# The attention layer's VectorE order: the weighted values of tile t ahead of the low part of tile t-1

## The reference

```python
q = (rowEmb @ qTrans).reshape(-1, HEADS, head_dim)
k = (colEmb @ kTrans).reshape(-1, HEADS, head_dim)
v = (colEmb @ vTrans).reshape(-1, HEADS, head_dim)
att = jnp.clip(jnp.einsum('ehd,ehd->eh', q, k), -10.0, 10.0)
expAtt = jnp.exp(att)
attNorm = segment_sum(expAtt, rows)[rows]
att = expAtt / (attNorm + 1e-08)
out = segment_sum((att[:, :, None] * v).reshape(-1, EMB), rows)
```

## Time and profile before

| | |
|---|---|
| median of 3 runs | 1238.45 us (1238.22 to 1241.88) |
| the profiled execution | 1255.07 us |
| its span, first to last instruction | 1253.3 us |
| attention tiles, first VectorE one-hot to the joining of the sums | 703.5 to 958.4 us |
| TensorE busy | 967.4 us, 77% |
| VectorE busy | 961.5 us, 77% |
| ScalarE busy | 600.1 us, 48% |
| GpSimd busy | 662.5 us, 53% |

### The profile page before, as it was taken

The page is one execution under the profiler, slowest core; times in us unless marked ns, Lnnn a source line. Parts: engine busy times, 40 slices in busy tenths (PEclk is TensorE's granted clock), DMA queues, the critical chain, the costliest instruction groups (busy, mean ns, idle before and its releaser), DMA issues.

```text
span 1253.3 us, 32626 instructions
## 1 busy us (share of the span) xinstructions
PE 967.4 (77%) x12003; PEld 732.8 (58%) x12003; DVE 961.5 (77%) x1247; ACT 600.1 (48%) x1503; POOL 662.5 (53%) x446
## 2 busy tenths in 40 slices
PE   4967577887999999999994767877772777727773
PEld 3645456776444544545543667877772777727763
DVE  8887878888565555565446499999998689978996
ACT  5531027777111111111101477878784389838984
POOL 1008888888788888888788889988100000000000
PEclk9977786555999999999995688888896589978998
DMA  8643214555222222222303388777834877728774
GB/s 167 130 104 74 53 28 165 191 191 153 57 71 69 83 70 69 83 70 83 67 2 111 117 275 276 265 270 267 301 137 172 341 289 282 279 83 291 282 299 137
DMA packets 73565, 202.18 MB, mean 161 GB/s; under 512 B 36667, under 2 KB 37467, under 8 KB 73509
## 3 DMA queue, kind: packets, MB, share of 16 engines
q1 hardware_dynamic: 57300, 186.25, 41.3%
q10 hardware_dynamic: 2465, 13.60, 4.8%
q0 software_dynamic: 13744, 1.59, 4.1%
HBM read 155.30 MB, written 45.63 MB: 160 GB/s over the span
## 4 chain that ended last, share of the span: by engine, by line
PE 42%; DVE 34%; issue 15%; DMA 4%; ACT 3%; DVEq 2%; SPq 0%; ACTq 0%
PE ps L1640 24%; DVE arena L982 4%; PE ps L1592 4%; DVE arena L948 4%; DVE arena L936 4%; DVE arena L957 3%; PE ps L1495 2%; DVE arena L1032 2%; PE ps L1452 2%; DVE arena L962 2%; PE ps L1437 2%; DMA base_room<-ohd_table 2%; DVE h_room L962 2%; PE ps L1482 2%; DMA hl_room<-in_edge_attr_dram 2%
## 5 line engine op out<-in xcount | busy, mean ns | idle before, releaser
L561 POOL DMA_INDIRECT w_table<-wpa,slot_i x425 | 657.1, 1546 | 218.3 <-issue 218.3
L1640 PE MATMUL ps<-arena,hl_room 125*128 125x500 f16 (+1 forms) x1750 | 342.7, 352 | 2.6 <-DVE hl_room L1218 2.0
L1437 PE MATMUL ps<-arena 125*128 125x64 f16 (+1 forms) x3900 | 232.0, 211 | 87.4 <-ACT arena L606 52.5
L1640 PEld LDWEIGHTS ps<-arena,hl_room 125*128 125x128 f16 x1750 | 155.7, 97 | 162.6 <-issue 4.6
L1437 PEld LDWEIGHTS ps<-arena 125*128 125x128 bf16 x3900 | 178.8, 103 | 93.4 <-ACT arena L606 50.5
L701 ACT ACTIVATE part_room<-ps 128x500 f16<-128x500 f32 (+1 forms) x70 | 38.0, 543 | 306.6 <-PE ps L1640 247.4
L1227 DVE SCALAR_TENSOR_TENSOR part_room<-ps,part_room 128x500 f16<-128x500 f32 (+1 forms) x70 | 43.6, 622 | 149.2 <-ACT part_room L701 143.6
L1442 PE MATMUL ps<-arena 125*128 (+1 forms) x1300 | 136.1, 205 | 0.0
L606 ACT ACTIVATE arena<-ps 128x384 f32<-128x384 f32 x325 | 130.9, 504 | 7.9 <-PE ps L1442 6.2
L632 ACT ACTIVATE arena<-ps,part_room 128x64 f32<-128x64 f32 x500 | 107.9, 339 | 18.6 <-PE ps L1437 10.9
L1442 PEld LDWEIGHTS ps<-arena 125*128 125x128 bf16 x1300 | 114.7, 108 | 0.5
(11 more groups left out here) (266 smaller groups left out, 1468.6 us busy)
## 6 DMA issues: line engine op xcount, KB each, us to landing
hl_room<-slot_rows SPq DMA_DIRECT2D x49, 832.0 KB, 4.3
arena<-slot_rows SPq DMA_DIRECT2D x38, 832.0 KB, 15.8
arena<-ohd_table SPq DMA_DIRECT2D x26, 832.0 KB, 5.0
arena<-ohs_table SPq DMA_DIRECT2D x25, 832.0 KB
base_room<-ohd_table SPq DMA_DIRECT2D x24, 832.0 KB, 5.9
hl_room<-in_edge_attr_dram ACTq DMA_DIRECT2D x17, 750.0 KB
ohs_table<-xs_room SPq DMA_DIRECT2D x25, 448.0 KB
ohs_table<-xs_room SPq DMA_DIRECT2D x25, 384.0 KB
```

Of the source, the lines that this page charges most:

```text
L561: pool.indirect_dma_start(w_table, bass.IndirectOffsetOnAxis(slot_i[:, u:u + 1], 0), wpa[:, u], None).then_inc(S[f"w_out{g % 2}"], 16)
L1437: last = pe.matmul(ps[:, m % RING, o:o + b - a], slots[:, k * L:(k + 1) * L], rhs, start=(i == 0), stop=(i == 1))
L1640: last = pe.matmul(ps[:, c, 0:w], hl[0:P, u, s, :], adj[:, s, c * CH * P:c * CH * P + w], start=(s == 0), stop=(s == T - 1))
```

## The change

In `layer1`, the four lines of the low part move from ahead of the weighted values to behind them. After the clamp of tile t, VectorE now comes first to the weighted values of tile t, with their waits for `l1_exp` and `l1_low`, and then to the low part of tile t-1, with its wait for `l1_high`. No instruction is added or removed, all waits keep their values, and no other engine's code changes.

```diff
                         vec.tensor_scalar(logit, logit, bound[:, 0:1], bound[:, 1:2], ALU.max, ALU.min).then_inc(S["l1_logit"], 1)
-                    if 3 in on:
-                        vec.wait_ge(S["l1_high"], s - 2)
-                        vec.scalar_tensor_tensor(msg1[:, 1 - par, :, M1:], msg1[:, 1 - par, :, 0:M1], HSCALE, G1m[1 - par],
-                                                 ALU.mult, ALU.subtract).then_inc(S["l1_low"], 1)
                     if 2 in on:
                         vec.wait_ge(S["l1_exp"], s - 1)
                         vec.wait_ge(S["l1_low"], s - 1)
                         vec.tensor_tensor(G1m[par][:, :, 0:D].rearrange("p c (a d) -> p c a d", a=HEADS),
                                           G1[:, par, :, D:2 * D].rearrange("p c (a d) -> p c a d", a=HEADS),
                                           exps.unsqueeze(3).to_broadcast([L, C, HEADS, HD]), ALU.mult
                                           ).then_inc(S["l1_val"], 1)
+                    if 3 in on:
+                        vec.wait_ge(S["l1_high"], s - 2)
+                        vec.scalar_tensor_tensor(msg1[:, 1 - par, :, M1:], msg1[:, 1 - par, :, 0:M1], HSCALE, G1m[1 - par],
+                                                 ALU.mult, ALU.subtract).then_inc(S["l1_low"], 1)
```

## The result

The changed kernel is slower. Its median over five runs is 1252.91 us (1249.60 to 1256.35), that of the kernel before, over five runs with the first three among them, 1241.88 us (1238.22 to 1244.62). The ratio is 1.0087, with a 95% interval of 1.0052 to 1.0121, about 11 us. The forecast was 12.0 us more, 1.0%, at 1250.4 us in a range of 1246.5 to 1254.

What follows compares the result with a forecast made beforehand. VectorE was taken to bound the kernel: 23 exposed waits of 0.53 us give 12.2 us, less 0.2 in the tail, so 12.0 on the median of 1238.45, 1250.4 us. The ends were 1247.5 to 1251.6, widened to 1246.5 to 1254.

Steps and rivals of the forecast that it cites:

- the tail: After step 26's clamp: the last low part comes 1.3 us earlier, but two back-to-back scatters on TensorE leave 0.2 us returned.
- the sum: 23 waits, 12.2 us, less 0.2 us returned at the end: 12.0 us, added to the median of 1238.45 us.
- The full engine: VectorE, busy 203.56 of 205 us at 9.55 us a step: a wait put into its sequence has nothing to hide in.
- The exposed wait: VectorE after each clamp: weighted values start after 0.78 us instead of 0.25, so 0.53 us a step, 12.2 us over 23.
- The covers: In the loop: the later low part keeps 3.2 us of slack before its scatter, and the product's row copies end in time.
- The bound of 1.3: Microseconds returned after the last clamp if TensorE were not in the way; used for the range's lower end, 1247.5 us.
- The profiled total: The whole profiled execution should go from 1255.07 to about 1267 us.
- rival 1: At the clamp on VectorE: the wait is covered after all, kernel not slower, 1237.2 to 1238.3 us; chance 0.03.
- mild form: At the clamp: some 0.2 of the 0.53 us come from profiling, leaving 7.4 us, so 1245.9 us; chance 0.06.
- rival 3: Low part late for its scatter, gathers and row copies set the step; several microseconds a step, above 1300 us; chance 0.02.
- rival 2: GpSimd comes first in the gap after the clamp: 0.66 us more in 16 steps, 10.6 at most, 1261.0 us; chance 0.05.

Runs made afterwards that it cites:

- e1: Kernel before, old order, with one added wait for the exponential ahead of the low part, nothing moved; ratio 1.0119 to the kernel before.
- e4: Changed kernel with the exponential computed twice by ScalarE, the first into an unused tile; ratio 1.0138 to the kernel before.
- e2: Changed kernel with the second one-hot moved from ahead of the clamp to between clamp and weighted values; ratio 1.0019 to the kernel before.
- e3: Kernel before, with the new order in step 26 alone, the last with weighted values; ratio 0.9998 to the kernel before.
- e6: e3 plus 140 unused matmuls on TensorE ahead of the last two scatters; 1237.92 us, ratio 0.9965 to the kernel before.
- e7: Changed kernel plus 100 unused matmuls on TensorE ahead of the last two scatters; ratio 1.0065 to the kernel before.
- e5: Kernel before, old order, with the exponential computed twice by ScalarE, the first into an unused tile; ratio 1.0020 to the kernel before.

## Why the prediction was right

The direction, the cause and the size of the wait held, and one term, the tail, did not. The kernel was 11.0 us slower where 12.0 were forecast, and the forecast ratio of 1.0097 lies in the measured interval. The time of 1252.91 us lies in the range only because this was widened for noise: it is above 1251.6, the upper end that the sum gave, since the three runs to which the sum was added had a median 3.43 us below that of all five. Point by point:

**The full engine.** Every step lost what was put into VectorE's sequence, and every run with another addition paid for it in the same way (0.53 in e1, 0.27 in e4, 0.12 in e2). Nothing absorbed it.

**The exposed wait.** 0.78 us from clamp to weighted values was read from step 2 and came out as 0.78 in all steps. From step 2's clamp to step 26's the time went from 947.00 - 721.50 = 225.50 us to 942.96 - 705.11 = 237.85, 12.35 more against 12.2.

**The covers.** ScalarE's idle before the high part vanished as said, and no wait of TensorE for the low part appeared in the loop. The low part ends at 817.94 + 2.00 = 819.94 and the scatter that needs it starts at 822.54:

```profile
822.54 1.70 PE L1452 MATMUL ps<-arena 128*128 128x136 f16 x26
```

That is 2.6 us of slack, where 3.2 were worked out from another step's scatter. One scatter was too few: in the loop's steps the slack runs from 1.41 us (low part done at 809.86, scatter at 811.27) to 3.11, and in the kernel before from 3.8 to 5.4, of which the prediction read one, 4.96. The cover held, with less than half of the margin that was claimed for it.

**The tail** is the term that was mis-sized: 0.2 us were to come back, and it was 11.35 - 10.18 = 1.17. The order of events was as described, down to the two scatters back to back. The step that failed put 3.11 us on each of them, from rows at the 1.2 GHz level; the second, which began near 950.6, was granted 0.97 of full speed from 951.6 to 952.8, and the pair took 5.15 us in place of 6.22. In e3, where both stayed near the lower level, the tail gave 0.30, and with both at the higher level 8.65 us remain. The bound of 1.3 that was kept for the range covered 1.17 by luck: it stood for a TensorE that is not in the way, and it is no bound either, as e6 and e7 give back 2.70, the 1.3 and the 1.41 by which a scatter is shorter at the higher level (3.11 - 1.70). By the prediction's own terms the 0.2 is 0.1 (951.67 + 6.22 = 957.89 against 958.00), which changes nothing.

**The profiled total** did not go to about 1267. Adding the sum to one profiled execution assumed that the next one would spend the same time in the earlier stages, and the next one reached L1640 12.9 us earlier and step 2's clamp 721.50 - 705.11 = 16.39 us earlier. What could be tested in the profile was the stage, and the sum there came out at 11.2 against 12.0.

**The rivals.** A covered wait (rival 1) is excluded by the step of 10.08 us. Its mild form, that profiling stretches the hand-over, would give 7.4 us, a ratio of 1.0060, which the interval of the changed kernel still holds. What speaks against it is e1, where 24 x 0.33 = 7.9 us would be 1.0064 and the interval begins at 1.0083. A late scatter (rival 3) did not occur. GpSimd (rival 2) did not hold up the weighted values: the steps are 10.08 us while its DMAs run and after their end at 825. It seems to hold up VectorE a little, though: in e2 the step is 9.71 us while its indirect DMAs run, 9.75 in the step of its last instruction at 823, and 9.67 behind it, and the one-hot behind the clamp takes 1.11 to 1.12 us, then 1.16, then 1.08:

```profile
881.26 0.33 DVE L952 TENSOR_SCALAR arena<-arena,bound 128x104 f32<-128x104 f32 x1
881.51 1.08 DVE L936 TENSOR_SCALAR arena<-arena,lane 125x3328 bf16<-125x3328 bf16 x1
882.51 1.88 DVE L958 TENSOR_TENSOR arena<-arena 128x1664 f32<-128x1664 f32 x1
```

If that is the mechanism of rival 2, it is worth 0.04 us a step and not the 0.66 that bounded it. The Trainium skill, "SBUF — State Buffer", section "Who interferes with whom", says of VectorE's two-port modes that whoever issues first gets the port pair shared with GpSimd for the whole instruction. No run here shows VectorE waiting for the 1.19 us that a GpSimd instruction takes when undisturbed.

## What to carry to other kernels

On an engine that is full, an instruction between a producer's hand-over and the use of what comes back is a cover, and its price is known before it is moved: the round trip from the start of the handed-over instruction to the start of the user, less the step to the next instruction. A step of the same loop that lacks the cover, here step 2, often shows that round trip already. Where TensorE idles ahead of the last matmuls of a stage, price them at both clock levels, as bounds, and compare profiles by the stage, not by their totals.

## What the runs showed of the hardware beyond this

In the changed kernel GpSimd also got through its work sooner. In a step before, three of its indirect DMAs were issued, one of them 5.73 us long; in a step after, five, none above 2.28 us:

```profile
803.22 1.18 POOL L561 DMA_INDIRECT w_table<-wpa,slot_i  x1 [0.30 <-issue]
804.70 1.71 POOL L561 DMA_INDIRECT w_table<-wpa,slot_i  x1 [0.31 <-issue]
806.72 2.28 POOL L561 DMA_INDIRECT w_table<-wpa,slot_i  x1 [0.30 <-issue]
809.30 1.61 POOL L561 DMA_INDIRECT w_table<-wpa,slot_i  x1 [0.30 <-issue]
811.22 1.78 POOL L561 DMA_INDIRECT w_table<-wpa,slot_i  x1 [0.31 <-issue]
```

Its last one began at 821.3 us instead of 875.6; counted from step 2's clamp, that is 116.2 us instead of 154.1. The longest DMA shrank by 3.5 us, far more than the 0.45 us of VectorE's gap. But the gap is not what it takes: e2, where VectorE shows no idle in these steps, issues five of them in a step too, the longest 2.21 us, and in e5, in the old order with a product that comes 0.14 us late, the long one takes 3.65 us instead of 5.74. Whether the order or some hundredths of a microsecond between VectorE's instructions let GpSimd in, these runs do not separate. Here nobody waits for it that early, so it bought nothing.

The second is the price of a dependence inside VectorE: an instruction that waits for the one just ahead of it started 0.11 to 0.12 us later than one that does not. From the reduce's start to the clamp it is 1.91 us in e2 and 939.19 - 937.27 = 1.92 in step 25 of the kernel before, from the product's start to the reduce 937.27 - 935.35 = 1.92, and 1.80 to a one-hot in either place. Both kernels, in which a one-hot stands between each such pair, avoid it in every full step.
